# A transformer block in one kernel: row work and weight loads moved between slots, and the joint products' copy and split moved forward

## What is computed

```python
h = _layernorm(x, ln1_g, ln1_b)
x = _attention(h, h, sa_wq, sa_wk, sa_wv, sa_wo, sa_bo) + x
h = _layernorm(x, ln2_g, ln2_b)
x = _attention(h, cond_emb, ca_wq, ca_wk, ca_wv, ca_wo, ca_bo) + x
h = _layernorm(x, ln3_g, ln3_b)
p = h @ ff_w1 + ff_b1
a, gate = (p[..., :D_FF], p[..., D_FF:])
h = a * jax.nn.gelu(gate, approximate=False) @ ff_w2 + ff_b2
return h + x
```

## Time and profile before

| what | us |
|---|---|
| median of 3 runs | 1696.74 |
| lowest, highest run | 1695.99, 1697.89 |
| the profiled execution's own time | 1697.57 |
| its span from first to last instruction | 1695.8 |
| PE busy in the span | 1680.5 |
| DVE, ACT, POOL busy | 1396.4, 1247.5, 1079.5 |

### The profile page before, as it was taken

The page is one execution under the profiler, slowest core; times in us unless marked ns, Lnnn a source line. Parts: engine busy times, 40 slices in busy tenths (PEclk is TensorE's granted clock), DMA queues, the critical chain, the costliest instruction groups (busy, mean ns, idle before and its releaser), DMA issues.

```text
span 1695.8 us, 39063 instructions
## 1 busy us (share of the span) xinstructions
PE 1680.5 (99%) x11712; PEld 1560.7 (92%) x11712; DVE 1396.4 (82%) x2964; ACT 1247.5 (74%) x3379; POOL 1079.5 (64%) x1804
## 2 busy tenths in 40 slices
PE   8999999999999999999999999999999999999999
PEld 8999999999999999999999999999999998888888
DVE  8887888888888888889888888888888877656665
ACT  7788788888888888888888888888888886122221
POOL 7776577777766666787777777777777565231211
PEclk9999999999999999999999999999999999999999
DMA  7776677778766567887787878787776785212110
GB/s 214 183 180 161 171 208 190 204 198 211 196 176 159 153 167 200 230 222 185 190 209 196 205 196 210 193 210 182 197 177 176 192 211 139 69 50 72 64 40 26
DMA packets 301138, 288.91 MB, mean 170 GB/s; under 512 B 103425, under 2 KB 252033, under 8 KB 300929
## 3 DMA queue, kind: packets, MB, share of 16 engines
q1 hardware_dynamic: 247136, 273.29, 61.8%
q10 hardware_dynamic: 53792, 13.12, 3.5%
HBM read 82.98 MB, written 37.49 MB: 71 GB/s over the span
## 4 chain that ended last, share of the span: by engine, by line
PE 89%; DVE 3%; SPq 3%; issue 2%; POOL 1%; DMA 1%; ACT 1%; ACTq 0%; DVEq 0%; POOLq 0%
PE QKB L556 16%; PE PVB L638 13%; PE PTB L569 11%; PE WOP L620 10%; PE VB L491 8%; PE S L458 6%; PE S L459 6%; PE S L1282 5%; PE PTB L1282 5%; PE QKB L1304 3%; PE VB L1304 3%; PE QKB L538 2%; SPq L673 1%; SPq L675 1%; SPq L1616 1%
## 5 line engine op out<-in xcount | busy, mean ns | idle before, releaser
L780 ACT ACTIVATE PT<-S,NM 128x256 f32<-128x256 f32 x1024 | 471.9, 473 | 147.2 <-DVE NM L945 146.0
L889 DVE TENSOR_TENSOR PL<-PTB,PH 128x512 fp32r<-128x512 f32 x512 | 350.9, 686 | 128.2 <-ACT PH L813 127.9
L1143 POOL TENSOR_TENSOR ON<-ON,RB 128x256 f32<-128x256 f32 x256 | 188.1, 735 | 287.4 <-DVE ON L965 265.5
L945 DVE TENSOR_REDUCE NM<-S 128x2 f32<-128x512 f32 x512 | 327.3, 681 | 0.3
L813 ACT ACTIVATE PH<-PTB 128x1024 fp32r<-128x1024 f32 x256 | 264.3, 1032 | 67.9 <-PE PTB L569 66.3
L569 PE MATMUL PTB<-IDN,PT 128*128 128x128 f32 x2048 | 265.7, 273 | 0.1
L458 PE MATMUL S<-RX 128*128 128x256 f32 x1012 | 253.9, 283 | 0.8 <-DMA RX<-QKS 0.8
L459 PE MATMUL S<-RX 128*128 128x256 f32 x1012 | 253.7, 283 | 0.0
L556 PE MATMUL QKB<-HT,WQ 128*128 128x512 f32 x936 | 242.9, 394 | 0.9
L620 PEld LDWEIGHTS WOP<-WO,OT 128*128 128x128 f32 x1536 | 217.5, 190 | 20.1 <-POOL OT L1148 0.2
L569 PEld LDWEIGHTS PTB<-IDN,PT 128*128 128x128 f32 x2048 | 229.5, 140 | 1.1 <-issue 0.5
(11 more groups left out here) (163 smaller groups left out, 2918.7 us busy)
## 6 DMA issues: line engine op xcount, KB each, us to landing
RX<-QKS SPq DMA_DIRECT2D x506, 192.0 KB, 2.9
RX<-QKS SPq DMA_DIRECT2D x506, 128.0 KB, 2.8
RB<-denominators SPq DMA_DIRECT2D x512, 64.0 KB, 2.7
out_dram<-XR SPq DMA_DIRECT2D x32, 256.0 KB, 3.5
weights_qk<-SPL SPq DMA_DIRECT2D x32, 256.0 KB, 3.4
WQ<-weights_qk SPq DMA_DIRECT2D x32, 256.0 KB, 3.4
rows<-XN SPq DMA_DIRECT2D x24, 256.0 KB, 2.6
rows<-HF SPq DMA_DIRECT2D x23, 256.0 KB, 2.7
```

Of the source, the lines that this page charges most:

```text
L780: last = e.activation(PT[:, c % 2, j * S:(j + 1) * S], S1[:, i, qt * S:(qt + 1) * S], ACT.Exp, bias=NM[:, j:j + 1], accum_out=DEN[:, c % 2 ...
L889: e.tensor_tensor(PL[:, cols], PTB[:, i, :], PH[:, s % 2, cols].bitcast(F32), ALU.subtract).then_inc(a.dve_pl, 1)
L945: e.tensor_reduce(NM[:, i * TT:(i + 1) * TT], S1[:, i, :].rearrange("p (t s) -> p t s", t=TT), AX.X, ALU.max, negate=True).then_inc(a.dve_ ...
```

## The change

It moves work and adds two waits; the products, copies and sums are the same in number.

- In every slot with a joint product ScalarE's `act_copy_both` stands between the exponentials of the first and the second head (before: only in slots 25 to 28), and VectorE's `dve_split_both` stands before the residual sum and the row work (before: after `RDT`).
- `normalized_in`: sequences 6 to 15 are normalized one slot earlier, in slots 8n - 22.
- The chunk work of VectorE stands inside `dve_slot`, after `dve_rows` and before `RDEN`. Chunk 1's statistics move from slots 250 to 252 to slots 244 to 246, its normalization from step 3 into slots 249 to 252; SyncE stores its rows in slots 251 and 253, VectorE's transposes come in steps 3 and 4 (before 5 and 6), ScalarE's scaling in step 4 (before 6). ScalarE's copies into `XN` and `HF` (raw 4 and 5) wait for those stores, and the loads of chunk 1 into `STG` wait until step 1 has read it.
- SyncE: `BOUT` in slot 237 instead of 248; the `WV` loads in slots 246, 247, 254 and 257 instead of 246, 248, 254 and 256; the last quarter in slots 252, 253, 255, 256 instead of 252 to 255. In the first half the `WV` loads go from slots 120 and 128 to 119 and 129.
- TensorE's tail: `pe_gates(e, EARLY + 1)` before `pe_second(e, 1)`.
- At the start VectorE's value copies wait for an older value split (`v - 3`), as `VF` holds four.

```diff
+def normalized_in(c):
+    n = due(c, -2, 2)
+    if n and OLD // PAIRS + 2 <= n < B:
+        return n
+    n = due(c, -1, 2)
+    return None if n and OLD // PAIRS + 2 <= n < B else n
...
                     last.then_inc(a.act_exp, 1)
-                    if late and i == 0:
+                    if joint(c + LEAD) and i == 0:
                         act_copy_both(e, c + LEAD)
...
-            if joint(c + LEAD) and not late:
-                act_copy_both(e, c + LEAD)
...
-            if due(c, -1, 2):
-                e.wait_ge(a.dve_th, due(c, -1) - 1)
-                dve_normalize(e, sl, a, due(c, -1), (near(due(c, -1)),))
+            n = normalized_in(c)
+            if n:
+                e.wait_ge(a.dve_th, n - 1)
+                dve_normalize(e, sl, a, n, (near(n),))
...
+        def dve_ffn_rows(e, c):
...
+            if c == ATT - 12:
+                e.wait_ge(a.dve_xo, B + HOLD + 4)
+                dve_stats(e, zero_ffn, fs, 1, 0, 1)
+            if c == ATT - 11:
+                dve_stats(e, zero_ffn, fs, 1, 2, 3)
+            if c == ATT - 10:
+                dve_aggregate(e, zero_ffn, fs, 1)
+            if c == ATT - 7:
+                e.wait_ge(fs.s_ht, KD)
+            if ATT - 7 <= c < ATT - 3:
+                dve_normalize(e, zero_ffn, fs, 1, ROWS, (c - ATT + 7,))
...
-                sl.wait(e, a.pl_v, v)
+                sl.wait(e, a.pl_v, v - 3)
...
-            if late:
+            if joint(c + LEAD):
                 dve_split_both(e, c + LEAD)
             if c < ATT:
                 dve_sum(e, sl)
             dve_rows(e, sl)
+            dve_ffn_rows(e, c)
...
-            if joint(c + LEAD) and not late:
-                dve_split_both(e, c + LEAD)
...
             e.wait_ge(fs.pe_raw, n + 1)
+            if n in (4, 5):
+                e.wait_ge(d_fs[n - 4], 16 * 2)
...
                 e.wait_ge(d_fs[h], 16 * (chunk + 1))
+                if chunk == 1:
+                    e.wait_ge(fs.dve_hf, 2)
...
-            if c >= 0 and c % PAIRS == 6 and sl.has(c + PAIRS):
+            if c >= 0 and c % PAIRS == (6 if c >= PAIRS else 4) and sl.has(c + PAIRS):
...
-                if f == (2 if chunk else 3):
+                if f == 2 and chunk:
                     sl.wait(e, fs.s_ht, KD * (chunk + 1))
                     dve_normalize(e, sl, fs, chunk + 1, ROWS)
-                turn = f - (4 if chunk else 5)
+                turn = f - (4 if chunk else 3)
...
-            if sl.c == ATT - 3:
+            if sl.c == ATT - 9:
+                e.wait_ge(fs.dve_xn, 2)
                 pool_rstd(e, zero_ffn, fs, 1)
...
+                            turns = ((0, 1, 2, 3), (0, 1, 3, 4))[quarter - 2]
...
-                            if c == four + 2 + 2 * n:
+                            if c == four + 2 + (n if g == 0 else 3 * n):
...
-                if c == ATT - PAIRS:
+                if c == ATT - 19:
                     e.wait_ge(a.pl_xb, 2 * B)
                     e.dma_start(BOUT[:, :], ff_b2.partition_broadcast(P)).then_inc(d_bo, 16)
...
+                if c in (ATT - 5, ATT - 3):
+                    store_ffn_rows(1, (c - ATT + 5) // 2)
...
+            pe_gates(e, EARLY + 1)
             pe_second(e, 1)
-            pe_gates(e, EARLY + 1)
             pe_outputs(e, ATT - 2)
```

More of the change, by code:

```diff
@@ L935, in dve_rows @@
                 dve_aggregate(e, sl, a, due(c, -3))
+        def dve_ffn_rows(e, c):
+            if c == FFN_START - 16:
+                e.wait_ge(a.dve_xo, B + HOLD + 2)
+                dve_stats(e, zero_ffn, fs, 0, 0, 1)
+            if c == FFN_START - 15:
+                dve_stats(e, zero_ffn, fs, 0, 2, 3)
+            if c == FFN_START - 14:
+                dve_aggregate(e, zero_ffn, fs, 0)
+            if c == FFN_START - 12:
+                e.wait_ge(a.s_ht, 4 * B)
+                e.wait_ge(a.pl_ct, 2 * B)
+            if FFN_START - 12 <= c < FFN_START - 8:
+                dve_normalize(e, zero_ffn, fs, 0, ROWS, (c - FFN_START + 12,))
+            if FFN_START - 6 <= c < FFN_START - 4:
+                dve_ffn_turn(e, 0, c - FFN_START + 6)
+            if c == ATT - 12:
[9 more added lines that the diff above has]
+                dve_normalize(e, zero_ffn, fs, 1, ROWS, (c - ATT + 7,))
         def dve_slot(e, sl):
@@ L1690, in fill_weights @@
                             at = j - LEAD + 2
+                            turns = (0, 1, 2, 3)
                         for chunk in range(4):
-                            if c == at + chunk:
+                            if c == at + turns[chunk]:
                                 if chunk == 0:
@@ L1774, in _ @@
                 if chunk + 1 < NCK:
-                    store_ffn_rows(chunk + 1, 0, 1)
+                    if chunk:
+                        store_ffn_rows(chunk + 1, 0, 1)
                     load_ffn_rows(e, chunk + 1, *range(8))
```

21 lines of the change are left out of this document (removed).

## The result

Before 1696.74 us (median, 1695.89 to 1698.22, 5 runs), after **1691.15 us** (1688.74 to 1692.19, 5 runs); ratio 0.9961, 95% interval 0.9950 to 0.9972. The change makes the kernel faster by 0.4%, 5.6 us in the first set and 7.2 us in the second. The profiled execution of after is the fastest of its five, with a span of 1686.9, and the profiled execution of before lies 0.8 above its median, so the two traces are 8.9 us apart, more than the medians are. The traces of the experiments tell much of what is the change and what is chance.

What follows compares the result with a forecast made beforehand. TensorE, busy 99% of the span, was taken as the bound. Gains of 3.8 + 0.5 + 0.7 + 0 + 1.0 + 0.5 + 2.3 = 8.8 us gave 1688.0 us, range some 3 us below to 1692.5.

Steps and rivals of the forecast that it cites:

- A: Self-attention, slots 36 to 116: 11 losses of 0.35 us vanish with the split before the row work; gain 3.8 us.
- The copy before the second head: ScalarE's copy between the heads' exponentials in joint slots: waits for nothing, 1.4 us left as cover; cost 0.
- Slower: Rival, chance 0.03: the copy waits so long that exponentials miss the next scores in some 54 slots; 16 us, 1704.
- B: Slot 127: with the split ahead TensorE's wait goes, gain 0.5 us; the same move gives 0 in cross-attention.
- C: First slots: the value copy waits for a GpSimd split three older; gain 0.7 us, bounds 0 and 1.0.
- D: Slots 232 to 249: scores about 1.0 to 1.2 us late, some 1.5 of late row work escaped, both absorbed; net 0.
- E: Slot 251: the scores' wait for their ring copy goes as `BOUT` and `WV` leave the queue; gain 1.0 us.
- F: Slot 253: `PVB` no longer starts late behind VectorE's statistics and aggregation; gain 0.5 us.
- G: Tail: gate product 0.95 us ahead, wait for chunk 1's split gone, new loss of 0.7; gain 2.3 us.

Runs made afterwards that it cites:

- old_order: The changed kernel with the copy again behind all four exponentials and the split again behind the row work; 1690.48 us, ratio 0.9954.
- repeat: The changed kernel once more without any edit, for a second trace; 1690.14 us, ratio 0.9956.
- no_loads: The changed kernel with `BOUT` and the weight loads (`WV`, last quarter) in their old slots; 1690.18 us, ratio 0.9955.
- copy_only: The kernel before with only ScalarE's copy of the joint product moved between the heads' exponentials; 1698.36 us, ratio 1.0007.
- before_again: The kernel before once more without any edit, for a second trace; 1696.95 us, ratio 0.9998.
- norm_only: The kernel before with only the normalization of sequences 6 to 15 one slot earlier; 1693.79 us, ratio 0.9981.
- rows_only: The kernel before with only the feed-forward part's chunk work moved, with its stores, scaling and TensorE's swap; 1693.95 us, ratio 0.9979.
- order_only: The kernel before with only the copy and the split of the joint product moved; 1694.3 us, ratio 0.9982.
- tail: hybrid with VectorE's step 4 before the last residual sum, chunk 1's scaling after gelu 5, `pe_outputs(ATT - 2)` before `pe_second(e, 1)`; 1686.06 us, ratio 0.9931.
- split_only: The kernel before with only VectorE's split moved ahead of the residual sum and row work; 1698.48 us, ratio 1.0008.
- hybrid: The changed kernel with the moved copy and split in self-attention only, old places in cross-attention; 1688.71 us, ratio 0.9947.
- tail2: The kernel tail with both transposes of chunk 1's turned rows in step 4; 1686.46 us, ratio 0.9929.

## Why the prediction came out as it did

**A, right in size, and not in what it takes.** 3.8 forecast; 3.9 to 4.2 measured. But the prediction named the split ahead of the row work as the cause and costed the moved normalization at nothing. Added to before one by one, either takes 3.2 or more: the order alone takes all of it (499.72, as with both), the normalization alone 0.8 less. Taken out of the changed kernel, the order gives back 0.8 (old_order). So beside the moved normalization, copy and split are worth 0.8 in self-attention, and cost 1.2 in cross-attention.

**The copy before the second head, cost 0: wrong.** The step that failed is "So it waits for nothing". It was read in slot 43, whose copy has a wait for a ring copy too, but there the ring copy had landed in time. In cross-attention it had not: the copy waits 0.56 in slot 131 and 0.85 in slot 171 of after, 1.14 in slot 171 of repeat and 1.40 in slot 155 of no_loads. In the eight traces with copy and split in the old place it waits there 0.18 at most. Two engines stand behind the copy. One is VectorE, which the prediction did not follow: its split, now directly behind the sums, waits for the copy, and sum, normalization and next maxima come late with it. The other is TensorE's scores, which wait for the second head's exponentials. The 1.4 us that the prediction found as cover held in slot 43 and in nearly all other slots, but not in these two, of no_loads and of repeat:

```profile
880.26 0.35 PE L467 MATMUL S<-RX 128*128 128x256 f32 x1 [0.30 <-ACT PT L789]
```

```profile
1084.69 0.36 PE L467 MATMUL S<-RX 128*128 128x256 f32 x1 [0.55 <-ACT PT L789]
```

Ahead of the first, at the end of slot 155, stands the wait of 1.40 for a ring copy; slots 155 and 156 lose 0.46 and 0.59. Ahead of the second no ring copy was late. In slot 193 ScalarE was issuing four loads of the context:

```profile
1077.89 2.63 ACTq L708 DMA_DIRECT2D XN<-in_ctx_dram  x2
1080.63 0.38 ACT L765 ACTIVATE ON<-PVB 64x256 f32<-64x256 f32 x1 [1.72 <-issue]
```

Its exponentials began 3.5 us into the slot instead of 1.7 to 2.2, and the slot takes 6.05 instead of 5.33. The copy between the two heads puts the second pair back by 0.5 of these 0.7 (an estimate, from the distance of the copy's start to the next exponential's).

The mechanism is that of the last rival (*Slower*), in single slots instead of 54, and its price is 1.2 us in the mean instead of 16. Its condition was put too rarely, too: the kernel has the wait before every even product, in 108 slots, and not in one of four. What the 1.2 us consist of is shown in part: in after 0.5 of the 1.0 lost stand right behind such a wait, in copy_only 0.1 of 1.2. B's sentence that the move "gives 0" in cross-attention is wrong with it.

**B, 0.5: chance.** The second trace of before has the slot at 5.35, and in none of the five other traces with the split behind the row work (before_again, norm_only, old_order, rows_only, copy_only) do slots 126 to 128 take more than 16.05. One trace cannot tell a stall of the kernel from one of the execution where a DMA ended the wait.

**C, 0.7: right.** The seven traces without the new wait take 220.8 to 221.5 to slot 36, the seven with it 220.1 to 220.6; the means differ by 0.7. TensorE's wait in slot 0 is gone in after.

**D, 0: wrong, with the wrong sign for its visible cost.** Slots 231 to 249 win 1.2 against the second trace of before and 1.9 against the first. The stall of about 1.0 at slot 240 did not come: ScalarE's copy in slot 239 of after waited 0.25, not 0.67, as the ring copy that it waits for landed 2.4 us before the first scores of slot 240, not 0.7:

```profile
1326.97 0.60 ACT L745 ACTIVATE QKS<-QKB 128x512 fp32r<-128x512 f32 x1 [0.25 <-issue]
```

Part of this was chance of the first trace of before: in before_again the ring copy lands 1.5 us ahead of slot 240 and the copy waits for nothing, and in order_only, with the copy ahead and the chunk work where it was, it lands 2.3 us ahead and there is no wait and no stall either. The lateness was also overstated: the scores of slot 240 start at 1334.35 in before and not at 1334.0, which leaves 0.8 to 0.9. The prediction took the ring copy's landing as given and moved only the copy toward it. Yet the queue issues ring copies behind its waits for VectorE's `RDT`; with the chunk work ahead of the reciprocals VectorE is in time at each slot's end, and the queue is likely to gain as well. That this chain is what wins the 1.2 is argued and not shown by itself. rows_only shows the same 102.11 without any other part of the change; that it is the place within the slot and not chunk 1's earlier statistics was not taken apart. By the rule of the Trainium skill ("DMA: Bandwidth & Descriptors", section "Issuing engines are not separate DMA queues") the prediction had an estimate of 0.7 by bytes: the landing came earlier, not later, and no_loads, which takes those bytes out of the stretch, is at the same 102.11, so nothing of that cost reaches TensorE here; it does not speak against the rule itself.

**E, 1.0: right in the traces**, 0.96 measured, and 1.35 when the loads alone are put back; but rows_only has it without the moved loads. **F, 0.5: off the sum.** The statistics no longer hold up slot 253 (4.88 instead of 5.53 us), but slot 254 then waits for the ring copy of 255 and takes 0.65 longer; stretch 251 to 254 is at 21.31 for 21.40. In the eight traces with the statistics moved it takes 20.70 to 21.74, 21.2 in the mean, by how late that ring copy lands; in the six others 21.38 to 21.40. The prediction looked for ring copies as a wall at slot 246 and not at 255:

```profile
1410.06 0.39 PE L467 MATMUL S<-RX 128*128 128x256 f32 x1 [0.49 <-DMA RX<-QKS]
```

**G, 2.3: 1.45 measured.** The step that failed is "the gate product moves 0.95 us ahead": counted from the first scores of slot 255 it starts at 25.48 instead of 25.58, 0.1 ahead (0.3 in repeat), and the whole 1.57 stays in front of it. The wait for chunk 1's split is gone, and the new loss at the gate product between is there (0.33 in brackets, 0.5 by the distances, 0.7 forecast). Missed was a new wait in front of them, 0.47 of the last attention output for GpSimd's `OT`, and 0.3 more at the product `PVB` ahead of it (0.44 in brackets, 0.15 before). In the kernel tail, where VectorE does step 4 before the residual sum, that gate product starts 1.2 sooner than in after.

By the first two traces the sum comes out at 8.9 for 8.8 forecast. That agreement is luck: -1.0 in cross-attention and the short terms F and G are offset by D's 1.9 and C's 1.0, and B's 0.5 and 0.7 of D's 1.9 are not the change's. The medians are 5.6 and 7.2 apart. The means of two traces of each kernel (start 0.9, self-attention 4.1, cross-attention -1.7, slots 231 to 249 1.6, slot 250 1.0, tail 1.5) give 7.4, with slot 127 left out.

## What to carry to other kernels

When a wait is put further ahead on an engine, ask who waits for that engine's result, and follow that second engine to its next deadline: the slack of the one that was moved says nothing of the other's. Two remedies for one stall may each suffice, so that their sum is not the sum of their gains; add each alone to the old kernel, and take each alone out of the new one. And before costing a stall of less than a microsecond behind a DMA, take a second trace of the same kernel: here 1.2 us that the first trace of before showed as losses were gone from the second.

## What the runs showed beyond that

The granted clock of TensorE fell for a short stretch in the tail of some executions and not of others. In norm_only, TensorE's gate product that follows the stall of 1.57 us took 4.61 us; the same product takes 3.02 in after:

```profile
1438.38 4.61 PE L1292 MATMUL S<-HT,WQ 128*128 128x512 f32 x12 [1.57 <-DVE PT L1422]
```

Busy by window of norm_only, the clock in the third column from the end:

```profile
1420.00:1438.50 18.50, 16.29 (x107) 14.35 (x106) 16.20 (x27) 8.01 (x14) 9.60 (x13) 1.00 0.22 69
1439.00:1442.00 3.00, 3.00 (x8) 2.30 (x7) 1.30 (x2) 0.00 (x0) 0.00 (x0) 0.50 0.46 131
1443.00:1460.00 17.00, 15.18 (x95) 13.56 (x95) 9.94 (x17) 4.88 (x7) 5.96 (x6) 1.00 0.00 0
```

The clock is at its full level (2.4 GHz), then at 0.50 (1.2 GHz), then back. TensorE was busy 16.3 of the 18.5 us ahead and had just stood for 1.57. copy_only and old_order show the same behind their stalls of 1.57, order_only behind its later stall of 1.82. Both traces of before, with the same stalls of 1.57 and 1.82, stayed at 1.00. The tails of norm_only, order_only and copy_only are 279.7 to 279.8, and 278.1 to 278.4 in the three traces of the same tail without the fall: a cost of 1.4 us that comes or not. (In old_order the tail is 277.38, against 276.7 to 276.9 of the same tail.)

The runs without a trace show it as well. The four traced executions with such a fall have a mean granted clock of 0.999, the ten without it 1.000. Of the 72 runs of before that were made beside the experiments 34 have 0.999, with a mean of 1698.7 us, and 38 have 1.000, with 1696.8. So it is a part of the spread of 4 to 5 us between these runs. It also enters a comparison of kernels: the eight runs of the changed kernel at 1.000 (of after and repeat) have a mean of 1690.4, 6.4 us below those 38 of before.

It became rarer as the stalls in the tail became shorter. Of the runs of kernels with the tail of before (before, before_again, order_only, norm_only, copy_only, split_only) 63 of 124 have a mean clock below 1.000; of those with the tail of the change (after, repeat, old_order, no_loads, rows_only, hybrid) 11 of 36; of tail and tail2 none of 10. No experiment changed a stall and nothing else, so the stalls as the cause are not shown by themselves.
